# A four-block graph network on one core: offsets loaded one by one eight chunks ahead, ScalarE's share from the fourth group, early counts and weighting on VectorE

## The chip, the core and the metric

One core of one Trainium2 chip. The metric is the device time in microseconds of one execution; for each kernel the median of several runs is given. Engines are called TensorE (PE in the rows; its weight loads PEld), VectorE (DVE), ScalarE (ACT), GpSimd (POOL) and SyncE (SP). Each has a sequencer of its own that takes its instructions in order; rows of a sequencer have a small q behind the engine (PEldq is TensorE's).

## The reference, cut to what matters

x is 512 nodes by 512 features. There are 16384 edges, sorted by dst, each with src, dst, one of 4 types and a weight. Four blocks of graph network follow one another, each in the form x = x + block(relu(layernorm(x))):

```python
h = x @ W + b                                  # block 0, diffusion
adj = 1 where an edge joins two nodes, either way, plus the identity; rows divided by their sum
out = dw[0] * h
for i in range(3):
    cur = adj @ cur                            # cur starts as h
    out = out + dw[i + 1] * cur
return relu(out)
# block 1: per type r: segment_sum((x[src] @ W_rel[r] + b_rel[r]) * weight), two layer norms, a gelu MLP
# block 2: normalised adjacency @ (x @ weight) + bias
# block 3: two SAGE layers, means over incoming edges
```

The edges enter all of this only through five 512 x 512 matrices: for each of the four types the sum of the weights of the edges from one node to another, and the number of edges. Block 0 needs the last one (the counts).

## The kernel before, in words

`build_matrices` turns the edge list into the five matrices in SBUF (`wall`, the counts at index R = 4), and beside that normalises x and multiplies it by block 0's W. `run_blocks` then computes the four blocks. The change lies in the first and at the head of the second.

**Chunks.** The edges are taken in 128 chunks (CH) of 128. As they are sorted by dst, a chunk touches few destination nodes: a window of 8 columns (WIDE) beginning at an offset that the chip works out from the chunk's first dst. VectorE makes, for a group of 16 chunks (G), one-hot matrices by comparison with an iota (`hot`, L375): `lo_hot` (src within its tile of 128), `key_hot` and `cnt_hot` (tile of src, type, and dst within the window). It multiplies `lo_hot` by the weight, which is split into three bf16 parts (V = 3; `weigh`, L381). The one-hots of three groups (RING) fit at a time, so group g waits for the chunks of group g - 3 (`chunk_done`). ScalarE makes the third weighted part for the first 8 chunks (BY_ACT) of groups 1 to 7 (`weigh_some`, L273), 8 activations a group; VectorE does the rest. Group 7 is made in two halves (`last_hots`).

**TensorE, per chunk** (`chunk`, L555): three matmuls with the weighted one-hots as stationary operand (L560, 128 columns) and one with `lo_hot` for the counts (L562, 32 columns). They add into PSUM at a place that is known only at run time: a register holds the chunk's offset, and two register instructions a chunk (FUSED_REGOPS) make the addresses from it. The registers are filled by TENSOR_LOAD instructions that read the offsets from SBUF (`off_row`): before the change one load of 16 registers at the head of each group, L569, eight in all. Behind it on TensorE's sequencer come the waits for the group's one-hots: L578 is the wait on `act_hots_ready`.

**Blocks.** The 512 destination columns lie as 32 blocks of 16 (DB) in the eight PSUM banks, in turn. A block's bank is zeroed by a matmul (L552) when it opens, one every fourth chunk, after its forerunner was copied. ScalarE copies each finished block to `wall` (L279) and its overlap with the next to `tails` (L281), in the order of closing; VectorE adds the tails, four blocks at a time (`add_tails`, L421). The last block is copied by VectorE (L454).

**From counts to hops.** `cnt_r` is a rounded copy of the counts. For the first 384 columns ScalarE makes it (`keep_early_counts`, L267), called between the block copies 28 and 29 in its order, after VectorE's sixth `add_tails` (semaphore `half_built`); the last 128 columns are VectorE's (L500). TensorE adds the counts to their transposes (L623, L617 for the early ones, L629 to L633 for the late). VectorE makes the adjacency of it (`symmetric`, L946), and the hops of block 0 begin (L1116). Before L946, VectorE sums dw (L955), scales b0 by it (L956) and weights the first two tiles of the projection (`weigh_projection`, L950); the other two tiles follow later.

**Order of the start.** VectorE works out keys and offsets, then checks that the edges suit this scheme (L339 to L345; if not, a slow branch with `slow` set runs instead, which these inputs don't take), then takes the moments of the first two tiles of x (`moments`, L312). TensorE turns the plan (L520 to L522) once the checks are done, spins ten matmuls (L507), transposes the first normalised tile (L529), spins six, and multiplies by W (L539; each of the matmuls stands as two rows). Every engine that branches loads the flag first, with a TENSOR_LOAD of one register (L77).

Of the kernel before, what the change touches and what calls it, by code (L numbers as in the profile page):

```python
# [17 lines left out]
F32 = mybir.dt.float32  # L18
# [9 lines left out]
P = 128  # L28
# [17 lines left out]
BY_ACT = 8  # L46
OUT_R = R + 1
# [7 lines left out]
def gnn_program(nc, x_in, src_in, dst_in, typ_in, wgt_in, w0_in, b0_in, dw_in, wself_in, bself_in, wrel_in, brel_in,  # L55
                g1_in, be1_in, g2_in, be2_in, wf1_in, bf1_in, wf2_in, bf2_in, w2_in, b2_in,
                wl1_in, bl1_in, wr1_in, wl2_in, bl2_in, wr2_in, out):
    with ExitStack() as keep:
# [17 lines left out]
        def load_flag(engine, kind):  # L76
# [15 lines left out]
        b0_loaded = sem("b0_loaded")  # L92
        half_built, built, early_kept, late_kept = sem("half_built"), sem("built"), sem("early_kept"), sem("late_kept")
# [4 lines left out]
                       both_ways, bias, inv_cnt, hi[0], lo[0], ident_r, cnt_r, b0, b0_loaded, half_built, built, early_kept, late_kept,  # L98
                       proj_out, hi_ready, lo_ready, sym_ready, x_in, src_in, dst_in, typ_in, wgt_in, w0_in, b0_in)
        run_blocks(nc, sem, block, wall, x, ident, ones, eye, eps, load_flag, psum, slots, h, h_t, adj, cnt_r, both_ways, bias,  # L100
                   inv_cnt, hi, lo, b0, b0_loaded, built, proj_out, hi_ready, lo_ready, sym_ready,
# [5 lines left out]
def build_matrices(nc, sem, sb, block, wall, x, ident, ones, eye, eps, slow_flag, load_flag, banks, psum, slots, h, h_t,  # L107
                   both_ways, bias, inv_cnt, hi0, lo0, ident_r, cnt_r, b0, b0_loaded, half_built, built, early_kept, late_kept,
# [22 lines left out]
    if True:  # L131
# [91 lines left out]
        def _(act):  # L223
# [72 lines left out]
            with act.If_ne(slow, 0):  # L296
                keep_early_counts()

        @block.vector
        def _(dve):  # L300
# [36 lines left out]
            dve.scalar_tensor_tensor(key, high_i, float(R * WIDE) / P, key, ALU.mult, ALU.add).then_inc(keys_ready, 1)  # L337
            dve.wait_ge(const_ready, 1)
# [8 lines left out]
            moments(0)  # L347
            moments(1)
# [5 lines left out]
            scale_and_shift(0)  # L354
# [35 lines left out]
            def hots(g):  # L390
# [8 lines left out]
                weigh(g, V - 1, slice(BY_ACT // 2, G // 2))  # L399
# [15 lines left out]
            def add_tails(q):  # L415
# [6 lines left out]
                                         ALU.add)  # L422

# [6 lines left out]
            with dve.If_eq(slow, 0):  # L430
# [26 lines left out]
            with dve.If_ne(slow, 0):  # L457
# [34 lines left out]
                for m in range(NT):  # L492
                    split_projection(m)
                dve.wait_ge(slow_cnt_out, NT)
# [844 lines left out]
```

## Time and profile before

| | |
|---|---|
| median of 3 runs | 386.02 us (385.9 to 386.74) |
| the profiled execution's own time | 385.97 us |
| its span, first to last instruction | 384.0 us |
| TensorE busy | 366.3 us (95%) |
| VectorE busy | 179.7 us (47%) |
| ScalarE busy | 97.0 us (25%) |
| GpSimd busy | 57.9 us (15%) |
| granted TensorE clock | 0.999 |

The profiled execution lies within 0.1 us of the median; 1.97 us of it lie outside the span. Matmuls are pipelined, so that their rows overlap: the time from one start to the next tells the pace, not the duration of one. Times in rows are microseconds from the start of the span, unless ns is written.

### The profile page before, as it was taken

To read this page: it belongs to the slowest core of one execution; us is meant where nothing else is said; L and a number is where in the kernel's file an instruction comes from. 1 tells how busy PE (TensorE), PEld (TensorE's weight loads), DVE (VectorE), ACT (ScalarE), POOL (GpSimd) and SP (SyncE) were. 2 spreads that over 40 slices of the span, in tenths; PEclk is the share of its full clock that TensorE was granted. 3 is DMA by queue.
4 is the path that set the end of the run, shared out by engine and by line. 5 is a ranking of instruction groups with operands and counts; after the bars stand their busy time and mean duration, and the time that the engine had idled before them with its cause. 6 is when DMAs were issued, how large, how long until landed. Compare 5 with 4: busy or idle time off the path is not lost.

```text
span 384.0 us, 4240 instructions
## 1 busy us (share of the span) xinstructions
PE 366.3 (95%) x1554; PEld 204.5 (53%) x1554; DVE 179.7 (47%) x328; ACT 97.0 (25%) x230; POOL 57.9 (15%) x48
## 2 busy tenths in 40 slices
PE   7898877899999999999999999999999999999996
PEld 2447766788444444454444447544455747445642
DVE  5898998788831122237320332004685447212311
ACT  3449886332510000000000102321124270212000
POOL 5000000000589700010011001000211064000000
PEclk9999999999999999999999999999999999999999
DMA  7000000399100000029100018027333000000011
GB/s 242 32 0 4 2 2 2 131 294 340 59 2 0 0 0 0 0 98 357 66 0 0 2 30 183 6 39 124 58 50 62 0 0 2 0 0 0 2 55 55
DMA packets 43812, 22.05 MB, mean 57 GB/s; under 512 B 35536, under 2 KB 36048, under 8 KB 43792
## 3 DMA queue, kind: packets, MB, share of 16 engines
q1 hardware_dynamic: 43264, 20.85, 19.9%
q0 software_dynamic: 240, 0.79, 0.7%
q8 instruction: 14, 0.23, 0.2%
q10 hardware_dynamic: 288, 0.13, 0.1%
q14 instruction: 6, 0.05, 0.0%
HBM read 20.72 MB, written 1.05 MB: 57 GB/s over the span
## 4 chain that ended last, share of the span: by engine, by line
PE 83%; DVE 12%; ACT 2%; DMA 1%; issue 1%; DVEq 0%; ACTq 0%
PE bank L1116 46%; PE bank L1190 14%; PE bank L1309 7%; PE bank L1221 7%; DVE slots L375 4%; DVE slots L381 3%; PE bank L539 3%; PE bank L1104 2%; PE bank L560 2%; DMA bias<-in_edge_type 1%; PE bank L552 1%; DVE wall L421 1%; DVE stats L922 1%; DVE bias L312 0%; PE bank L1132 0%
## 5 line engine op out<-in xcount | busy, mean ns | idle before, releaser
L1116 PE MATMUL bank<-slots,h_t 128*128 128x512 f32 x192 | 83.6, 593 | 0.8 <-ACT h_t L845 0.8
L1116 PEld LDWEIGHTS bank<-slots,h_t 128*128 128x128 f32 x192 | 35.9, 190 | 43.6 <-issue 43.6
L1190 PE MATMUL bank<-slots,wall 128*128 128x512 f32 x128 | 55.7, 593 | 0.0
L560 PE MATMUL bank<-slots 128*128 128x128 bf16 x384 | 32.6, 220 | 7.5 <-ACT slots L273 4.6
L1190 PEld LDWEIGHTS bank<-slots,wall 128*128 128x128 f32 x128 | 24.0, 190 | 28.7 <-issue 28.7
L997 DVE TENSOR_TENSOR slots<-bank,bias 128x512 f32<-128x512 f32 x16 | 11.1, 691 | 43.9 <-PE bank L1116 43.9
L560 PEld LDWEIGHTS bank<-slots 128*128 128x128 bf16 x384 | 24.8, 97 | 10.9 <-issue 8.4
L1116 PE MATMUL bank<-wall,h_t 128*128 128x512 f32 x64 | 29.0, 593 | 0.5 <-ACT h_t L845 0.5
L1309 PE MATMUL bank<-wall,slots 128*128 128x512 f32 x64 | 28.4, 592 | 0.0
L1116 PE MATMUL bank<-h_t,slots 128*128 128x384 f32 (+2 forms) x96 | 28.0, 451 | 0.0
L1221 PE MATMUL bank<-slots 128*128 128x512 f32 x64 | 27.8, 592 | 0.0
L1116 PE MATMUL bank<-hi,adj 128*128 128x512 f32 x64 | 25.5, 399 | 1.1 <-DVE adj L946 1.1
L1116 PE MATMUL bank<-lo,adj 128*128 128x512 f32 x64 | 24.9, 390 | 0.0
L834 ACT ACTIVATE columns<-mean_var,eps 128x1 f32<-128x1 f32 x20 | 5.9, 293 | 74.7 <-DVE mean_var L923 74.6
L381 DVE TENSOR_TENSOR slots<-slots,inv_cnt 128x2048 bf16<-128x2048 bf16 (+1 forms) x26 | 24.4, 990 | 0.0
L375 DVE TENSOR_TENSOR slots<-inv_cnt,both_ways 128x2048 bf16<-128x2048 f16 (+3 forms) x27 | 21.9, 862 | 2.2 <-PE bank L562 1.7
L562 PE MATMUL bank<-slots 128*128 128x32 bf16 x128 | 22.7, 178 | 0.0
L1116 PEld LDWEIGHTS bank<-h_t,slots 128*128 128x128 f32 x96 | 15.7, 191 | 11.6 <-issue 7.7
L1221 PEld LDWEIGHTS bank<-slots 128*128 128x128 f32 x64 | 12.1, 190 | 14.8 <-issue 14.8
L1309 PEld LDWEIGHTS bank<-wall,slots 128*128 128x128 f32 x64 | 12.1, 190 | 14.5 <-issue 14.4
L1014 DVE SCALAR_TENSOR_TENSOR h<-bank,columns,h 128x512 f32<-128x512 f32 x4 | 3.0, 751 | 35.4 <-PE bank L1190 35.4
L795 POOL TENSOR_TENSOR h<-h,bias 128x512 f32<-128x512 f32 x4 | 5.1, 1264 | 95.2 <-PE bank L1104 95.2
(162 smaller groups left out, 454.6 us busy)
## 6 DMA issues: line engine op xcount, KB each, us to landing
slots<-in_L_gnn_W_rel SPq DMA_DIRECT2D x4, 1024.0 KB, 11.7
slots<-in_L_gnn_W_ffn SPq DMA_DIRECT2D x2, 2048.0 KB, 12.6
slots<-in_L_gnn_Wl SPq DMA_DIRECT2D x32, 64.0 KB, 2.5
slots<-in_L_gnn_Wr SPq DMA_DIRECT2D x32, 64.0 KB, 2.3
x<-in_x SPq DMA_DIRECT2D x4, 256.0 KB, 5.8
bias<-in_L_gnn_W SPq DMA_DIRECT2D x1, 1024.0 KB, 7.9
slots<-in_L_gnn_W_self SPq DMA_DIRECT2D x1, 1024.0 KB, 5.4
bias<-in_L_gnn_b_rel SPq DMA_DIRECT2D x4, 256.0 KB, 10.0
```

What stands on the lines that cost most here:

```text
L375: return dve.tensor_tensor(to[:, pairs], have, want, ALU.is_equal)
L381: dve.tensor_tensor(wgt_hot[:, s, v, pairs], lo_hot[:, s, pairs], by, ALU.mult).then_inc(hots_ready, 1)
L539: ins = pe.matmul(proj_bank[m], h_t[:, k, m * P:(m + 1) * P], w0[:, k, :], start=(k == 0), stop=(k == KT - 1))
L560: pe.matmul(place[:, :, 0:R, 0:WIDE], wgt_hot[:, s, v, a, :, j], key_hot[:, s, a, :, j], start=False, stop=False, skip_group_check=True)
L562: pe.matmul(place[:, :, R, 0:WIDE], lo_hot[:, s, a, :, j], cnt_hot[:, s, a, :, j], start=False, stop=False, skip_group_check=True).then_in ...
L834: act.activation(std[:, t:t + 1], mean_var[:, t, 1:2], ACT.Sqrt, bias=eps[:]).then_inc(std_ready[n], 1)
L997: dve.tensor_tensor(msg[r][:, m, :], main[m][:], brel[r], ALU.add).then_inc(msg_out, 1)
L1104: ins = pe.transpose(t_bank[use % 2][:, i * P:(i + 1) * P], b, ident[:])
L1116: ins = pe.matmul(bank, left, right, start=start and i == 0, stop=stop and i == len(pairs) - 1)
L1190: ins = pe.matmul(main[m][:], wall[:, r, s, tile(m)], msg[r][:, s, :], start=(r == 0 and s == 0), stop=(r == R - 1 and s == NT - 1))
L1221: ins = pe.matmul(main[m][:], hid[:, g, tile(m)], wf2[:, g, :], start=(g == 0), stop=(g == GT - 1))
L1309: ins = pe.matmul(sage_bank[m][:], agg_t[layer][:, k, tile(m)], sage(wl, k), start=False, stop=(k == KT - 1))
```

## The change

- TensorE loads each chunk's offset with a load of its own. The first eight (AHEAD) stand ahead of the first chunk; then the load for chunk c + 8 stands behind the matmuls of chunk c.
- ScalarE makes its part of the weighted one-hots from group 3 on (ACT_FROM); VectorE makes all of groups 0, 1 and 2. TensorE waits for ScalarE's part in groups 3 to 7 alone.
- The early counts' copy moves from ScalarE to VectorE, behind its sixth `add_tails`; the semaphore `half_built` goes.
- Summing dw, scaling b0 and weighting the first two tiles move from the head of `run_blocks` to VectorE's place behind the second `split_projection`, before the seventh `add_tails`. The fourth `split_projection` now follows the third.
- VectorE takes the moments of tiles 0 and 1 before the checks, and `scale_and_shift(0)` before it waits for the turned plan.

```diff
+ACT_FROM = 3
+AHEAD = 8
...
         @block.scalar
...
-            def keep_early_counts():
-                act.wait_ge(half_built, 1)
-                act.activation(cnt_r[:, :, most], wall[:, R, :, most], ACT.Copy).then_inc(early_kept, 1)
...
                 for g in range(1, CH // G + 1):
-                    if g < CH // G:
+                    if ACT_FROM <= g < CH // G:
                         weigh_some(g)
                     while kept < NB - 1 and closes(kept) < g * G:
                         keep_block(kept)
-                        if kept == NB - 4:
-                            keep_early_counts()
                         kept += 1
...
         @block.vector
...
             dve.scalar_tensor_tensor(key, high_i, float(R * WIDE) / P, key, ALU.mult, ALU.add).then_inc(keys_ready, 1)
+            moments(0)
+            moments(1)
             dve.wait_ge(const_ready, 1)
...
-            moments(0)
-            moments(1)
+            scale_and_shift(0)
 
             dve.wait_ge(plan_t_ready, 3)
...
-            scale_and_shift(0)
...
-                weigh(g, V - 1, slice(BY_ACT // 2, G // 2))
+                weigh(g, V - 1, BACK if g >= ACT_FROM else WHOLE)
...
+            def keep_early_counts():
+                dve.tensor_copy(cnt_r[:, :, most], wall[:, R, :, most]).then_inc(early_kept, 1)
+
+            def weigh_bias():
+                dve.wait_ge(dw_loaded, 16)
+                dve.wait_ge(b0_loaded, 16)
+                link(dve.tensor_reduce(dw_sum[:], dw[:], AX.X, ALU.add))
+                link(dve.tensor_scalar(b0[:], b0[:], dw_sum[:], None, ALU.mult))
+
+            def weigh_projection(m):
+                dve.scalar_tensor_tensor(h[:, m, :], h[:, m, :], dw[:, 0:1], b0[:], ALU.mult, ALU.add).then_inc(acc_ready, 1)
...
-                add_tails(NB // 4 - 3).then_inc(half_built, 1)
-                for m in range(NT - 1):
+                link(add_tails(NB // 4 - 3))
+                keep_early_counts()
+                for m in range(2):
                     split_projection(m)
+                weigh_bias()
+                for m in range(2):
+                    weigh_projection(m)
                 add_tails(NB // 4 - 2)
-                split_projection(NT - 1)
+                split_projection(2)
+                split_projection(3)
...
         @block.tensor
...
+            def offset(c):
+
+                return nc.values_load_multi_w_load_instructions(
+                    off_row[0:1, c:c + 1], [PE], min_val=0, max_val=7 * N + DB - 2,
+                    skip_runtime_bounds_check_because="masked to that on the chip")[1][0]
+
...
+                at = [offset(c) for c in range(AHEAD)]
                 for g in range(CH // G):
-                    at = nc.values_load_multi_w_load_instructions(
-                        off_row[0:1, g * G:(g + 1) * G], [PE], min_val=0, max_val=7 * N + DB - 2,
-                        skip_runtime_bounds_check_because="masked to that on the chip")[1]
                     for c in range(g * G, (g + 1) * G):
...
-                            pe.wait_ge(act_hots_ready, BY_ACT * g)
+                            if g >= ACT_FROM:
+                                pe.wait_ge(act_hots_ready, BY_ACT * (g - ACT_FROM + 1))
...
-                        chunk(c, at[c % G])
+                        chunk(c, at[c])
+                        if c + AHEAD < CH:
+                            at.append(offset(c + AHEAD))
...
@@ run_blocks, head of VectorE's program
-            dve.wait_ge(dw_loaded, 16)
-            dve.wait_ge(b0_loaded, 16)
-            dve.wait_ge(proj_out, NT)
-            link(dve.tensor_reduce(dw_sum[:], dw[:], AX.X, ALU.add))
-            link(dve.tensor_scalar(b0[:], b0[:], dw_sum[:], None, ALU.mult))
-            for m in range(2):
-                weigh_projection(m)
             for t in range(NT):
                 symmetric(t)
```

## Rows read from the trace of the kernel before

**Rows 1.** The page's part 4, the chain that ended last, by engine.
```profile
PE 83%; DVE 12%; ACT 2%; DMA 1%; issue 1%; DVEq 0%; ACTq 0%
```

**Rows 2.** Groups by line, TensorE, 28 to 71 us: busy, mean ns, idle before and releasers.
```profile
L560 PE MATMUL bank<-slots 128*128 128x128 bf16 x384 | 32.6, 220 | 7.5 <-ACT slots L273 4.6 <-issue 1.8 <-DVE slots L375 1.1
```

**Rows 3.** TensorE's sequencer by line: ns min/median/max, first and last start; then 42.6 to 45.
```profile
L569 PEldq TENSOR_LOAD <-both_ways x7: 1102/1103/1112, 31.9 to 64.7; - x7
...
L578 PEldq EVENT_SEMAPHORE  x8: 51/51/51, 25.9 to 65.8; - x8
...
L569 PEldq TENSOR_LOAD <-both_ways x1: 1104/1104/1104, 42.7 to 42.7; - x1
...
L578 PEldq EVENT_SEMAPHORE  x1: 51/51/51, 43.9 to 43.9; - x1
...
L560 PEldq FUSED_REGOPS  x3: 42/42/42, 44.0 to 44.5; - x3
```

**Rows 4.** Timeline of TensorE, groups 0 and 7: start us, duration us.
```profile
29.12 0.33 PE L560 MATMUL bank<-slots 128*128 128x128 bf16 x3
...
29.32 0.33 PE L560 MATMUL bank<-slots 128*128 128x128 bf16 x3
...
69.98 0.18 PE L562 MATMUL bank<-slots 128*128 128x32 bf16 x1
...
70.23 0.18 PE L562 MATMUL bank<-slots 128*128 128x32 bf16 x1
```

**Rows 5.** Loads of one register on TensorE's sequencer, the two L77.
```profile
L77 PEldq TENSOR_LOAD <-slow_flag x1: 493/493/493, 23.9 to 23.9; - x1
...
L77 PEldq TENSOR_LOAD <-slow_flag x1: 307/307/307, 72.5 to 72.5; - x1
```

**Rows 6.** Timeline of VectorE, 32 to 70 us.
```profile
32.64 2.70 DVE L375 TENSOR_TENSOR slots<-inv_cnt,both_ways 128x2048 bf16<-128x2048 f16 x3 [1.67 <-PE bank L562]
...
60.29 1.89 DVE L381 TENSOR_TENSOR slots<-slots,inv_cnt 128x1024 bf16<-128x1024 bf16 x3
...
68.92 0.66 DVE L421 TENSOR_TENSOR wall<-wall,bias 128x480 f32<-128x480 f32 x1 [2.99 <-ACT bias L281]
```

**Rows 7.** Timeline of ScalarE, 68 to 71 us.
```profile
68.78 1.49 ACT L267 ACTIVATE cnt_r<-wall 128x1536 fp32r<-128x1536 f32 x1
```

**Rows 8.** The chain that ended last, 72 to 76 us: start, us, what.
```profile
73.03 1.42 DVE h L950 x2
74.45 0.62 DVE adj L946 x2
```

**Rows 9.** Timeline of TensorE, 70 to 76 us.
```profile
70.89 0.41 PE L623 MATMUL bank<-cnt_r,ident_r 128*128 128x384 f32 x1 [0.49 <-issue]
...
72.78 0.50 PE L629 MATMUL bank<-cnt_r,ident_r 128*128 128x128 f32 x3
...
75.11 0.50 PE L1116 MATMUL bank<-hi,adj 128*128 128x512 f32 x1 [1.15 <-DVE adj L946]
```

**Rows 10.** Timeline, 6 to 17 us, and the request of x's second tile.
```profile
6.60 0.69 DVE L312 BATCH_NORM_STATS2 bias<-x 128x6 f32<-128x512 f32 x1
...
8.22 0.25 DVE L352 CAST both_ways<-bank 1x128 int32<-1x128 f32 x1
...
7.21 2.32 PE L507 MATMUL bank<-both_ways 128*128 128x512 bf16 x10
...
11.88 1.96 PE L539 MATMUL bank<-bias,h_t 128*128 128x512 f32 x4 [0.17 <-ACT h_t L235]
...
16.89 1.98 PE L539 MATMUL bank<-bias,h_t 128*128 128x512 f32 x4 [0.90 <-ACT h_t L235]
...
L197 SPq DMA_DIRECT2D x<-in_x x1: 432/432/432, 2.1 to 2.1; - x1
...
DMA to landing us min/median/max: 3.5/3.5/3.5
```

**Rows 11.** Timeline of TensorE, 1 to 5 us.
```profile
1.32 3.48 PE L507 MATMUL bank<-both_ways 128*128 128x512 bf16 x8 [1.32 <-POOL both_ways L205]
```

More of the change, by code:

```diff
@@ L91, in gnn_program @@
         b0 = sb("b0", [P, D], F32)
-        b0_loaded = sem("b0_loaded")
-        half_built, built, early_kept, late_kept = sem("half_built"), sem("built"), sem("early_kept"), sem("late_kept")
+        dw = sb("dw", [P, HOPS + 1], F32)
+        dw_sum = sb("dw_sum", [P, 1], F32)
+        b0_loaded, dw_loaded, acc_ready = sem("b0_loaded"), sem("dw_loaded"), sem("acc_ready")
+        built, early_kept, late_kept = sem("built"), sem("early_kept"), sem("late_kept")
         proj_out, hi_ready, lo_ready, sym_ready = sem("proj_out"), sem("hi_ready"), sem("lo_ready"), sem("sym_ready")
@@ L97, in gnn_program @@
         build_matrices(nc, sem, sb, block, wall, x, ident, ones, eye, eps, slow_flag, load_flag, banks, psum, slots, h, h_t,
-                       both_ways, bias, inv_cnt, hi[0], lo[0], ident_r, cnt_r, b0, b0_loaded, half_built, built, early_kept, late_kept,
+                       both_ways, bias, inv_cnt, hi[0], lo[0], ident_r, cnt_r, b0, dw, dw_sum, b0_loaded, dw_loaded, acc_ready, built, early_kept, late_kept,
                        proj_out, hi_ready, lo_ready, sym_ready, x_in, src_in, dst_in, typ_in, wgt_in, w0_in, b0_in)
         run_blocks(nc, sem, block, wall, x, ident, ones, eye, eps, load_flag, psum, slots, h, h_t, adj, cnt_r, both_ways, bias,
-                   inv_cnt, hi, lo, b0, b0_loaded, built, proj_out, hi_ready, lo_ready, sym_ready,
+                   inv_cnt, hi, lo, b0, dw, dw_loaded, acc_ready, built, proj_out, hi_ready, lo_ready, sym_ready,
                    dw_in, wself_in, bself_in, wrel_in, brel_in,
@@ L107, in build_matrices @@
 def build_matrices(nc, sem, sb, block, wall, x, ident, ones, eye, eps, slow_flag, load_flag, banks, psum, slots, h, h_t,
-                   both_ways, bias, inv_cnt, hi0, lo0, ident_r, cnt_r, b0, b0_loaded, half_built, built, early_kept, late_kept,
+                   both_ways, bias, inv_cnt, hi0, lo0, ident_r, cnt_r, b0, dw, dw_sum, b0_loaded, dw_loaded, acc_ready, built, early_kept, late_kept,
                    proj_out, hi_ready, lo_ready, sym_ready, x_in, src_in, dst_in, typ_in, wgt_in, w0_in, b0_in):
@@ L291, in _ @@
                         keep_block(kept)
-                        if kept == NB - 4:
-                            keep_early_counts()
                         kept += 1
-            with act.If_ne(slow, 0):
-                keep_early_counts()
         @block.vector
@@ L493, in _ @@
                     split_projection(m)
+                weigh_bias()
+                for m in range(2):
+                    weigh_projection(m)
                 dve.wait_ge(slow_cnt_out, NT)
-                dve.memset(stats[:, 0, 0:1], 0.0).then_inc(half_built, 1)
+                keep_early_counts()
                 dve.memset(stats[:, 1, 0:1], 0.0).then_inc(built, 1)
@@ L691, in run_blocks @@
         bf1 = sb("bf1", [P, GT], F32)
-        dw = sb("dw", [P, HOPS + 1], F32)
-        dw_sum = sb("dw_sum", [P, 1], F32)
         dw_inv = sb("dw_inv", [P, HOPS, NT], F32)
@@ L699, in run_blocks @@
         rows_loaded, rel_rows_loaded, late_rows_loaded = sem("rows_loaded"), sem("rel_rows_loaded"), sem("late_rows_loaded")
-        dw_loaded, bf1_loaded = sem("dw_loaded"), sem("bf1_loaded")
+        bf1_loaded = sem("bf1_loaded")
         wself_loaded, w2_loaded = sem("wself_loaded"), sem("w2_loaded")
@@ L722, in run_blocks @@
         inv_root_ready, inv_cnt_ready = sem("inv_root_ready"), sem("inv_cnt_ready")
-        acc_ready, hop_ready = sem("acc_ready"), sem("hop_ready")
+        hop_ready = sem("hop_ready")
         self_ready, self_out, msg_ready, msg_out, agg_ready, agg_out = (
```

2 lines of the change are left out of this document (1 added, 1 removed).

## The prediction

> **What bounds the kernel now.** I read the chain first, for where time can be won or lost at all: TensorE carries 83% of it [rows 1]. The change touches two stretches, the chunk stage (28 to 70 us) and the handover to the hops (70 to 75 us), plus some reordering ahead of 10 us; from 75.11 on nothing changes, so that part only shifts.
>
> In the chunk stage the groups by line show 384 L560 matmuls busy for 32.6 us with 7.5 us of idle before them [rows 2], put down to ScalarE or VectorE. Those two had long been done: the idle sits at each group's start, where TensorE's sequencer loads 16 offsets (L569). From 31.9 on there are seven such loads, 1.103 us each [rows 3]. One boundary tells the rest: load at 42.7 for 1.104 us, then the wait L578 at 43.9, then the register arithmetic (FUSED_REGOPS) of the next chunk at 44.0 [rows 3]. L578 uses none of the loaded registers and its semaphore was satisfied long before, yet it starts only after the load. So **a load holds everything behind it on that sequencer**. From the load's start to the register arithmetic it is 1.3 us; less 1.104 and L578's 0.051 that leaves two steps between instructions of some 0.07 us; I reckon with 0.06.
>
> The sequencer also paces the chunks. In group 0, where it had run ahead while the projections kept the array busy, chunks follow at 0.20 us (29.12, 29.32). In the last group, without zeroing between them, they follow at 0.25 us (69.98, 70.23) [rows 4]. The array needs 0.20, the sequencer 0.25: it has no slack, and whatever is added to it lengthens the stage.
>
> **Offsets one by one.** The change removes 8 loads of 16 registers and adds 128 loads of one. Eight stand ahead of the first chunk and 120 come right behind a chunk's matmuls. "Eight ahead" helps only if the sequencer goes on while a load is under way, which rows 3 speak against. What does a load of one register cost? L77 is one, twice on TensorE's sequencer: 0.493 us at 23.9, the first load of the program there, and 0.307 us at 72.5 [rows 5]. Bounds: below, a cost purely by registers, 1.103/16 = 0.069; above, 0.493. I take 0.307: it is the one that isn't the first of its kind, and a fixed part with a rate per register fits both sizes (0.307 + 15 x 0.053 = 1.10). With the step of 0.06 behind it a load adds 0.365 us, and a chunk goes from 0.25 to 0.61 us.
>
> The sum goes along the sequencer:
> - Leading loads: today's first starts near 24.7 (L578's first, 25.9, less one load and a step [rows 3]); 8 x 0.365 = 2.9 from there, to 27.6. The projections hold the array until 28.2, so they are covered; if they weren't, they would cost the difference to today's single load, 1.8 us.
> - First 16 chunks: 16 x 0.61 = 9.8 and some 0.1 for the zeroing, to 37.5. Today it is through with them at 31.9, and with the load and the wait behind it at 33.1: +4.4 us.
> - The other 112 chunks: 104 more loads x 0.365 = 38.0, less six removed loads of 1.16 = 7.0, less 0.2 for the waits L578 of groups 1 and 2: +30.8 us.
> - Together **+35.2 us**: the last chunk ends near 105.6 instead of 70.4.
>
> The ends of the price for a load: at 0.069 the 128 loads give 30.5 us less (390 in all), at 0.493 they give 23.8 more (444).
>
> The Trainium skill (DMA: Bandwidth & Descriptors, Latency and other measured facts) gives a floor of about 600 ns for a tensor_load. By it the time would be an estimated 458 us; the trace disagrees, with 307 and 493 ns for the same thing, and the rows decide.
>
> **ScalarE's share from group 3.** VectorE weighs the front half of groups 1 and 2 too: 2 x 0.6 us (three products take 1.89 at half size [rows 6]). It then stood idle for 1.67 us before group 3, waiting for chunks [rows 6]: covered today, and by far with chunks at 0.61. ScalarE loses 16 small activations in time that it doesn't need. Worth 0 here; without that cover it would be +1.2.
>
> **Early counts.** ScalarE's copy L267 (1.49 us at 68.78) held up the last two block copies [rows 7]. It goes to VectorE, which waited 2.99 us before 68.92 [rows 6]. No row has this form on VectorE: bounds 1.5 (what ScalarE takes) to 2.1 (L421, 0.66 for 480 elements a partition [rows 6], for 1536), both below 2.99, and the wait grows with slow chunks. Cost 0. The last block's tail is then added a little earlier, but TensorE's own work (L623, L617: 70.89 to 72.78 [rows 9]) is ready no sooner, being released by the end of the chunks and not by the counts.
>
> **Weighting early.** The bias scaling and two L950 (73.03 for 1.42 us) stand right before the first L946 in the chain [rows 8]. They move into VectorE's wait. L946 then waits for the first L629, which starts at 72.78 (three in 0.50 us [rows 9]): it starts at about 73.1 instead of 74.4. **-1.3 us**, bounds 0 (if the moved work lay exposed in its new place) and -1.6 (nothing between L500 and L946). Late next is L629, behind TensorE's counts. b0 and dw were asked for in the first microseconds, long before: no wait.
>
> **Moments before the checks.** VectorE does the two moments (6.60 to 8.22, 1.6 us [rows 10]) before the checks. x's second tile was asked for at 2.1 and took 3.5 to land: by 5.6, in time for its moments near 6.2. But the plan's matmuls wait for the checks, and behind them on TensorE are ten spins and the first transposes. Spins at 7.21 become 8.8 and the first L539 at 11.88 about 13.1. Four plus four of them with the transposes between take 4 us, so the second tile, today waiting 0.90 us for h_t until 16.89, starts at 17.05: **+0.2 us** (bounds -0.15 and +1.2).
>
> **Sum.** 35.2 - 1.3 + 0.2 = +34.1. The profiled execution took 385.97 (span 384.0, 1.97 outside it), level with the median of 386.02. Forecast **420 us**.
>
> **Rivals.**
> 1. *The load runs beside what follows* and only the use of the register waits; eight chunks ahead hides it. Then VectorE bounds: from 32.64 it works without a break until the last half group at 62.1 [rows 6], eight chunks of 0.25 end at 64.1, not 70.4. -6.3 - 1.3 + 0.2 = -7.4: 378.6 us. It decides the sign where a load holds the sequencer for less than 0.078 us (the 9.4 us otherwise saved, over 120). For it: the program is plainly written for that. Against it: L578 lies behind the load all eight times (25.9 to 65.8 [rows 3]). If a load still takes a step of 0.1, the time is about 389. Chance 0.10, of which 0.07 faster, 0.01 the same. The Trainium skill (Advanced Engine Details and Errata, Sequencer Loop) says that other engine instructions can be read and queued while a control instruction executes, which read widely is this rival; no row here shows it, since a chunk begins with register arithmetic, no engine instruction.
> 2. *A load is priced by its registers*: 0.07 to 0.2 us, 390 to 405 us. Against it: 0.307 for one register. Chance 0.04.
> 3. *TensorE's clock falls to 1.2 GHz*, as its array works 0.20 of each 0.61 us. Spins took 0.43 us each at the start (3.48 for 8) and 0.23 later (2.32 for 10) [rows 10, 11]. In the chunk stage 0.40 is still under 0.61; the count transposes (1.9 us) would double and the first hops run at half speed: +2 to +4, 422 to 424. It lies within the forecast, a quarter of it.
>
> The forecast's case, with a load between about 0.2 and 0.5 us, has 0.84; 0.02 is left for what I don't see, counted as slower but 0.01.
>
> **Numbers.** Range 410 to 440: a load of 0.23 (420 - 10) up to 0.46 (420 + 20), the clock included; outside lie rivals 1 and 2 and the outer price. Less than 0.2%, 0.8 us, can't be told from no change. Faster 0.07, same 0.02, slower 0.91.
>
> **What would show it.** 128 one-register loads near 0.31 us, register arithmetic 0.06 behind each; chunks 0.61 apart from the first to the 120th and 0.25 for the last eight; no pause at group boundaries; ScalarE and VectorE waiting on L562 throughout; TensorE idle two thirds of the stage; first hop 3.4 us behind the last chunk's end (70.4) where it was 4.7 (75.11 [rows 9]). Wrong if FUSED_REGOPS starts while a load is still open: then the stage is shorter than today's, VectorE has no idle in it, and rival 1 holds.

## The result, and the profile after

The changed kernel takes 422.91 us (median of 4 runs, 421.57 to 423.35) where the kernel before takes 385.96 in the same comparison: 1.0946 times as long, interval 1.0917 to 1.0976. The forecast was 420, range 410 to 440. The profiled execution took 421.57 us, its span 419.5, at a mean granted TensorE clock of 0.909 (before: span 384.0, 0.999). It is the fastest of the four: the median lies 1.3 us above it, and no trace shows where those are spent.

The page of the kernel after: part 1, the granted clock in 40 slices of part 2, and the chain by engine (rows 1 showed TensorE 83% and VectorE 12%).

```profile
PE 403.2 (96%) x1554; PEld 224.0 (53%) x1554; DVE 182.2 (43%) x329; ACT 91.9 (22%) x213; POOL 57.9 (14%) x48
...
PEclk9997555555899999999999999999999999999999
...
PE 93%; DVE 2%; issue 2%; ACT 1%; DMA 1%; ACTq 0%
```

VectorE has all but left the chain. The slices are 10.5 us wide: in the fifth to tenth, 42 to 105 us, the granted clock is half of full speed. That is nearly the whole chunk stage.

TensorE's sequencer, the loads by line over the whole run, then between 60 and 61.9 us, with the register arithmetic of the same stretch (ns min/median/max, first and last start):

```profile
L572 PEldq TENSOR_LOAD <-both_ways x128: 293/298/313, 25.4 to 103.8; - x128
...
L572 PEldq TENSOR_LOAD <-both_ways x3: 298/298/307, 60.2 to 61.4; - x3
...
L581 PEldq FUSED_REGOPS  x3: 42/42/42, 60.5 to 61.8; - x3
```

They alternate. Three loads start within 60.2 to 61.4, so one starts every 0.60 us, and the register arithmetic of a chunk (at 60.5 behind the load of 60.2) starts after each. The same stretch on the array, to be set against the pace of 0.25 in [rows 4]:

```profile
60.03 0.50 PE L581 MATMUL bank<-slots 128*128 128x128 bf16 x3
60.33 0.23 PE L583 MATMUL bank<-slots 128*128 128x32 bf16 x1
60.64 0.50 PE L581 MATMUL bank<-slots 128*128 128x128 bf16 x3
60.93 0.23 PE L583 MATMUL bank<-slots 128*128 128x32 bf16 x1
61.24 0.50 PE L581 MATMUL bank<-slots 128*128 128x128 bf16 x3
```

A chunk starts every 0.60 us. The groups by line and the waits of the stage, 28 to 108 us (waits: us in total, times, longest), say who follows whom:

```profile
L581 PE MATMUL bank<-slots 128*128 128x128 bf16 x384 | 58.6, 295 | 7.5 <-issue 3.6
...
ACT wall L279 <- PE bank L583: 47.8, 26, 3.0
DVE slots L370 <- PE bank L583: 23.1, 5, 6.8
PEld bank L581 <- issue: 18.5, 63, 0.4
```

ScalarE waits 47.8 us and VectorE 23.1 us for chunks to end; the weight loads wait 18.5 us for issue, that is, for nothing but their own sequencer. In the row of matmuls TensorE looks almost as busy as ever: idle before them is 7.5 us, the same as in [rows 2], and busy time has grown from 32.6 to 58.6. That is the trap of this profile. The matmuls are no more work; each is shown longer (295 ns against 220) at the lower clock, and the pipelined rows fill the gap that the loads make. The pace, not the busy share, shows the loss.

The last of the register arithmetic of the chunks, before (its L560) and after:

```profile
L560 PEldq FUSED_REGOPS  x128: 42/42/42, 26.0 to 69.9; - x128
```

```profile
L581 PEldq FUSED_REGOPS  x128: 42/42/42, 28.4 to 105.9; - x128
```

The sequencer reaches the last chunk 36.0 us later. At the end of the stage, the answer to [rows 9]:

```profile
106.95 0.23 PE L583 MATMUL bank<-slots 128*128 128x32 bf16 x1
107.02 0.67 PE L645 MATMUL bank<-cnt_r,ident_r 128*128 128x384 f32 x1
...
109.33 0.50 PE L651 MATMUL bank<-cnt_r,ident_r 128*128 128x128 f32 x3
...
110.40 0.50 PE L1129 MATMUL bank<-hi,adj 128*128 128x512 f32 x1
```

The last chunk ends at 107.18 (before 70.41) and the first hop starts at 110.40 (before 75.11): 3.22 us between them where there were 4.70. From the last chunk, +36.8, the handover gives back 1.5; 35.3 us are left at the first hop, and the span is 35.5 us longer.

### The profile page after: what moved, and what is told of

Its sections match the earlier page's. It is cut to its first block, busy times and chain, and to the rows that moved or that the text cites. A ratio compares the mean times of both kernels' runs of the same rounds, so it can differ in the third digit from the quotient of the medians.

```text
span 419.5 us, 4340 instructions
## 1 busy us (share of the span) xinstructions
PE 403.2 (96%) x1554; PEld 224.0 (53%) x1554; DVE 182.2 (43%) x329; ACT 91.9 (22%) x213; POOL 57.9 (14%) x48
## 4 chain that ended last, share of the span: by engine, by line
PE 93%; DVE 2%; issue 2%; ACT 1%; DMA 1%; ACTq 0%
PE bank L1129 42%; PE bank L1203 13%; PE bank L581 12%; PE bank L1322 7%; PE bank L1234 7%; PE bank L567 4%; PE bank L554 3%; PE bank L1117 2%; PE bank L522 1%; DMA bias<-in_edge_type 1%; PE bank L583 1%; DVE stats L942 1%; PE bank L544 0%; PE bank L1145 0%; PE bank L639 0%
## 5 line engine op out<-in xcount | busy, mean ns | idle before, releaser
L581 PE MATMUL bank<-slots 128*128 128x128 bf16 x384 | 58.6, 295 | 7.5 <-issue 3.6
L1129 PEld LDWEIGHTS bank<-slots,h_t 128*128 128x128 f32 x192 | 35.9, 190 | 43.6 <-issue 43.6
L581 PEld LDWEIGHTS bank<-slots 128*128 128x128 bf16 x384 | 33.4, 123 | 24.0 <-issue 18.5
L370 DVE TENSOR_TENSOR slots<-inv_cnt,both_ways 128x2048 bf16<-128x2048 f16 (+3 forms) x27 | 21.9, 863 | 23.7 <-PE bank L583 23.1
L583 PE MATMUL bank<-slots 128*128 128x32 bf16 x128 | 28.7, 224 | 0.0
L376 DVE TENSOR_TENSOR slots<-slots,inv_cnt 128x2048 bf16<-128x2048 bf16 (+1 forms) x26 | 25.5, 1033 | 0.0
L279 ACT ACTIVATE wall<-bank 128x320 f32<-128x320 f32 x31 | 13.4, 434 | 47.8 <-PE bank L583 47.8
```

The source lines that it names most:

```text
L279: act.activation(wall[:, :, :, b * DB:(b + 1) * DB].rearrange("p r t d -> p t r d"), block_of(b)[:, :, :, 0:DB], ACT.Copy).then_inc(block_ ...
L370: return dve.tensor_tensor(to[:, pairs], have, want, ALU.is_equal)
L376: dve.tensor_tensor(wgt_hot[:, s, v, pairs], lo_hot[:, s, pairs], by, ALU.mult).then_inc(hots_ready, 1)
L581: pe.matmul(place[:, :, 0:R, 0:WIDE], wgt_hot[:, s, v, a, :, j], key_hot[:, s, a, :, j], start=False, stop=False, skip_group_check=True)
L583: pe.matmul(place[:, :, R, 0:WIDE], lo_hot[:, s, a, :, j], cnt_hot[:, s, a, :, j], start=False, stop=False, skip_group_check=True).then_in ...
L1129: ins = pe.matmul(bank, left, right, start=start and i == 0, stop=stop and i == len(pairs) - 1)
```

## The experiments

The theory after the result: a load of one register holds TensorE's sequencer for 0.30 us and a step of 0.06, whatever is behind it and however far off its use. The rivals: the loss lies in another part of the change; the distance of eight chunks hides some of it; the lower clock makes it. Every kernel was compared with the kernel before on the same chip, whose medians lay between 385.96 and 386.11.

### Which part of the change costs it

The kernel after with only the loads of 16 registers back at the heads of the groups:

```diff
...
-                at = [offset(c) for c in range(AHEAD)]
+                cuts, at = [0, 16, 32, 48, 64, 80, 96, 112, 128], []
...
+                        if c in cuts:
+                            at += offsets(c, cuts[cuts.index(c) + 1] - c)
...
-                        if c + AHEAD < CH:
-                            at.append(offset(c + AHEAD))
```

> The changed kernel with the eight loads of 16 registers back at the groups' heads; all other parts of the change stay. Theory (a load holds TensorE's sequencer, the rest of the change is worth little): the chunk stage is back near 42 us, the handover keeps its 1.3 us gain, the start keeps the 0.8 us that the spins at half clock cost: 385.4 us, between 384.5 and 386.2. Rival (something else of the change, ScalarE's share or VectorE's added work, lengthens the stage): over 395 us.

Measured 386.35 us, 1.0004 times the kernel before (0.9992 to 1.0017): just above the range that was expected, and the rival, over 395, is out. And the other way round, the kernel before with nothing but the loads changed (edit as in the diff of the change: `offset`, the eight ahead, one behind each chunk):

> The kernel before with only the loads changed: one register each, eight chunks ahead. Theory: all of the loss is here. 120 chunks at 0.60 us in place of 0.25 and the 16-register loads gone: +36 us on the sequencer and about 0.8 for the array at half clock behind it: 422.5 us, between 421 and 424. Rival (the loss needs the other parts too): under 400 us.

Measured 422.29 us, 1.0938 (1.0917 to 1.0959). So all of the loss lies in the loads. Everything else in the change together makes no difference that these runs can tell from none, where 1.1 us had been forecast as its gain.

### Whether the distance hides anything

The kernel after with `AHEAD = 1` in place of 8:

> The changed kernel with AHEAD = 1: each offset is loaded one chunk ahead instead of eight. Theory (the sequencer stands still during a load, so the distance to its use hides nothing): the same time, 421.5 to 423. Rival (the load runs on its own, and the distance hides part of it): each chunk would wait for up to 0.25 us more, 452 us.

Measured 427.12 us (424.65 to 429.46), 1.1081. The total is a miss, but not by way of the distance. The register arithmetic of the chunks in this kernel:

```profile
L581 PEldq FUSED_REGOPS  x128: 42/42/42, 24.3 to 105.6; - x128
```

Its last starts at 105.6, with eight ahead at 105.9. The ends alone prove little, since the stage starts earlier here (zeroing at 27.41, not 28.93) and holds seven more loads. What decides is the pace: between 40 and 100 us both sequencers start 95 loads, so **the chunks come as fast without any distance**. The time is lost behind the stage. With eight ahead the last eight chunks have no load and follow more closely; with one ahead they too are 0.60 apart. In windows behind the stage (us; busy time and count of PE, PEld, DVE, ACT, POOL; granted clock; DMA share; GB/s) it shows:

```profile
106.00:109.00 3.00, 2.63 (x14) 2.47 (x12) 1.45 (x3) 0.60 (x2) 0.00 (x0) 0.50 0.21 17
109.00:112.00 3.00, 3.00 (x14) 2.90 (x15) 1.36 (x5) 0.00 (x0) 0.00 (x0) 0.50 0.92 325
112.00:116.00 4.00, 4.00 (x13) 3.23 (x13) 3.42 (x11) 0.00 (x0) 0.00 (x0) 0.61 1.04 291
```

and the same place in the kernel after:

```profile
104.00:108.00 4.00, 3.93 (x40) 3.78 (x37) 2.44 (x5) 1.81 (x6) 0.00 (x0) 0.51 0.01 4
108.00:112.00 4.00, 4.00 (x28) 3.68 (x27) 3.24 (x9) 0.00 (x0) 0.00 (x0) 1.00 0.51 187
```

At 1.2 GHz (0.50) through the count transposes and at 0.61 in the first hops, where the kernel after is back at 1.00 from 108 on. Its first hop starts at 112.10 instead of 110.40. The profiled execution (424.65) is the fastest of the four, so the trace says nothing on the 2.5 us between it and the median.

Then each offset loaded twice, with both registers in use (the second for the chunk's count matmul):

```diff
-            def chunk(c, at):
+            def chunk(c, at, again):
...
-                pe.matmul(place[:, :, R, 0:WIDE], lo_hot[:, s, a, :, j], cnt_hot[:, s, a, :, j],
+                pe.matmul(counted[:, :, R, 0:WIDE], lo_hot[:, s, a, :, j], cnt_hot[:, s, a, :, j],
...
+                            at.append(offset(c + AHEAD))
+                            twice.append(offset(c + AHEAD))
```

> The kernel before with one-register loads eight chunks ahead, each offset loaded twice: the first register addresses the three weighted matmuls, the second the counts' matmul, so that both loads are needed and both are far ahead of their use. Theory (a load holds the sequencer for 0.30 us and a step of 0.06 however far its use is): 120 x 0.36 = 43 us on top of only_loads (422.3): 465 us. Rival (what costs is waiting for the value, not the load): 422 to 425 us.

Measured 467.14 us (465.78 and 468.51), 1.2089 (1.2041 to 1.2137). The loads in it:

```profile
L558 PEldq TENSOR_LOAD <-both_ways x248: 294/302/313, 24.6 to 147.0; - x124
```

120 more loads than in the kernel that changes the loads alone, and the profiled execution is 43.6 us longer than that one's (465.78 against 422.16): 0.363 us a load, against 0.365 in the sum.

An earlier attempt at this, with a second load whose result nothing used:

> The kernel before with one-register loads eight chunks ahead, and behind each of the 120 a second load of one register that nothing uses. Theory (a load costs its 0.30 us and a step of 0.06 whether or not its value is waited for): 120 x 0.36 = 43 us on top of the kernel with the loads alone, 465 us. Rival (only the use of the register waits): about the same as with the loads alone, 422 us.

It took 423.24 us and is void: its trace has 128 loads of offsets, as many as without the edit, so the unused ones never ran. It says nothing on either theory.

### Whether an engine instruction can pass a load

The prediction's rival 1 had one reading that no row before could exclude: behind a load there was always register arithmetic or a semaphore, never an engine instruction alone. So the kernel before, with the load for chunk c + 8 between the first and the second matmul of chunk c. The weight load of the second matmul has a fixed address and needs no register.

```diff
+                    if v == 0 and c + AHEAD < CH:
+                        ahead.append(offset(c + AHEAD))
```

> As only_loads, but the load for chunk c + 8 stands between the first and the second matmul of chunk c. Theory (nothing behind a load is handed on before it ends, engine instructions included): the weight loads of the second matmul begin only after the load's end, some 0.35 us behind the first's; time 422 us as only_loads, or up to 1 us more. Rival (matmuls can be handed on while a load is under way): the second and third matmul follow the first at 0.06 to 0.11 us inside the load's duration, and the stage is up to 0.05 us a chunk shorter: 416 to 420 us.

Its profiled execution took 423.89 us; the other one took 437.77, far outside what these kernels otherwise scatter, and I draw nothing from it. The first is 1.7 above the profiled execution of the kernel that changes the loads alone, where at most 1 was expected and the rival wanted less time, not more. Two of its loads, and the weight loads in the same stretch (start us, us):

```profile
L558 PEldq TENSOR_LOAD <-both_ways x1: 299/299/299, 60.4 to 60.4; - x1
...
L558 PEldq TENSOR_LOAD <-both_ways x1: 299/299/299, 61.1 to 61.1; - x1
```

```profile
60.40 0.14 PEld L567 LDWEIGHTS bank<-slots 128*128 128x128 bf16 x1
60.73 0.14 PEld L567 LDWEIGHTS bank<-slots 128*128 128x128 bf16 x2 [0.19 <-issue]
60.88 0.10 PEld L571 LDWEIGHTS bank<-slots 128*128 128x128 bf16 x1
61.08 0.10 PEld L567 LDWEIGHTS bank<-slots 128*128 128x128 bf16 x1
61.44 0.14 PEld L567 LDWEIGHTS bank<-slots 128*128 128x128 bf16 x2 [0.25 <-issue]
```

The load of 60.40 lasts 0.30 us, and the next weight load starts at 60.73; the load of 61.1 is over at 61.41, and the next starts at 61.44. Before both the weight loads stand idle, 0.19 and 0.25 us, for nothing but issue. The whole trace agrees: of the 117 loads of offsets that start after 29.5 us, one has a weight load that starts inside it, 2 ns after its own start. So nothing new is handed to the array while a load is open; in the kernel after matmuls do start beside a load, but they stand ahead of it in the program. The Trainium skill (Advanced Engine Details and Errata, Sequencer Loop) says that other engine instructions can be queued while a control instruction executes; for a register load on TensorE this trace disagrees.

### What the lower clock costs

The kernel after with one matmul of zeros, 440 columns wide, added to the banks for each chunk below 112. It leaves the sums as they are and keeps the array busier without touching the loads.

```diff
+                if c < CH - G:
+                    pe.matmul(flat[:, bass.ds(at, NT * OUT_R * COLS)], zeros[:, 0:P], zeros[:, 0:NT * OUT_R * COLS],
+                              start=False, stop=False, skip_group_check=True)
```

> The changed kernel with one more matmul per chunk, for chunks 0 to 111: zeros by zeros, 440 columns, added at the chunk's place, so that TensorE's array works 0.38 of each 0.60 us instead of 0.20. Theory (the clock fell because the array idled behind the loads, and costs only the lag of the last chunks and the slow start of the handover, 1.1 us): granted clock at least 0.98 over the span, 440-column matmuls 0.18 us apart from what follows, 421 to 424 us, the gain of 1.1 given back by one more instruction a chunk. Rival (the clock falls all the same): 0.76 us of array work a chunk, 437 us or more.

Measured 422.02 us (421.6 to 423.74), 1.0935 (1.0899 to 1.0971). The stage in windows, first of the kernel after, then of this one:

```profile
28.00:40.00 12.00, 9.47 (x85) 6.13 (x84) 5.25 (x7) 3.08 (x9) 0.00 (x0) 0.84 0.00 1
40.00:52.00 12.00, 10.94 (x82) 7.48 (x81) 7.44 (x9) 5.17 (x18) 0.00 (x0) 0.50 0.01 2
```

```profile
28.00:40.00 12.00, 11.37 (x101) 6.98 (x100) 5.24 (x7) 3.08 (x9) 0.00 (x0) 1.00 0.01 1
40.00:52.00 12.00, 11.11 (x100) 6.83 (x101) 7.41 (x9) 4.97 (x18) 0.00 (x0) 1.00 0.01 2
```

With the array given more to do, the clock stays at 2.4 GHz (1.00) and the time is the same. So the clock fell because the array had so little to do between loads: here it fell at a pace of 0.60 us a chunk, and at the same pace with the added matmul it did not.

What its fall costs is small, and the medians (0.9 us apart, the runs of each spread over 2 us) can't tell it from nothing. In the traces the last register arithmetic of a chunk starts 0.9 us later than in the kernel after (106.8 against 105.9), which is the price of the added instructions, and yet the array ends the stage at the same time (107.24 against 107.18). So the low clock cost about 0.8 us there: the half-speed matmuls still fit between two loads, and only the last chunks lag.

### What the rest of the change is worth

The kernel after with the old loads, and the moments back behind the checks (the handover's edits kept):

```diff
-            moments(0)
-            moments(1)
             dve.wait_ge(const_ready, 1)
...
-            scale_and_shift(0)
+            moments(0)
+            moments(1)
 
             dve.wait_ge(plan_t_ready, 3)
...
+            scale_and_shift(0)
```

> The changed kernel with loads of 16 back and also the old order at the start (the checks before the moments of tiles 0 and 1, scale_and_shift(0) after the plan's copies). Left of the change: ScalarE's share from group 3, the early counts on VectorE, the early weighting. Theory (these give 1.3 us at the handover, and the new order at the start was what gave it back): 384.7 us, between 384.2 and 385.2. Rival (the start's order is worth nothing, and something else eats the 1.3 us): 386 us.

Measured 384.78 us, 0.9961 (0.9945 to 0.9978): 1.3 us faster than the kernel before. The handover here takes 3.37 us from the last chunk's end to the first hop, by its trace.

The opposite, the kernel before with only the moments ahead of the checks:

> The kernel before with only the new order at the start: the moments of tiles 0 and 1 ahead of the checks, scale_and_shift(0) ahead of the plan's copies. Theory (TensorE waits 1.6 us longer for the plan, its spins behind that wait run at half clock, and the first projection starts 1 to 3 us later, of which the second tile's wait for h_t absorbs a part): 1.6 us slower, as undo_loads stood to old_front: 387.6 us, between 387.0 and 388.1. Rival (the sum of the prediction, spins at full clock, +0.2): 386.2 us.

Measured 387.99 us, 1.0033 (1.0015 to 1.0051). Its runs spread from 386.50 to 388.90: the medians are 2.0 us apart, the ratio of all runs gives 1.3. The timeline of its TensorE, to be set against [rows 10], where ten spins took 2.32 us and the first projection started at 11.88:

```profile
7.93 0.37 PE L520 MATMUL bank<-ident,bias 128*1 128x128 f32 x1 [1.57 <-DVE bias L347]
...
8.81 4.43 PE L507 MATMUL bank<-both_ways 128*128 128x512 bf16 x10
...
15.06 1.45 PE L539 MATMUL bank<-bias,h_t 128*128 128x512 f32 x3
```

The plan's matmul waits 1.57 us for VectorE's checks, now behind the moments, and the ten spins after it run at half speed, 0.44 us each. The zeroing of the chunk stage then starts at 30.11 instead of 28.17. The change's two parts that look like reordering thus work against each other: the handover gives 1.3 us, the start takes 1.3 to 2.

### A version that is faster than both

Three more kernels start from the one with the old front. The first loads fewer times: 32 and 16 registers ahead of the first chunk, then 32, 32 and 16 at chunks 48, 80 and 112.

```diff
-                cuts, at = [0, 16, 32, 48, 64, 80, 96, 112, 128], []
+                cuts, at = [0, 48, 80, 112, 128], []
...
-                            at += offsets(c, cuts[cuts.index(c) + 1] - c)
+                            if c == 0:
+                                at += offsets(0, 32)
+                            at += offsets(len(at), cuts[cuts.index(c) + 1] - len(at))
```

> As old_front, with 5 loads of 32, 16, 32, 32 and 16 registers: the first two ahead of the first chunk, the others at chunks 48, 80 and 112. Theory (a load holds the sequencer for 0.245 us and 0.053 per register, and the sequencer sets the stage's pace): loads of 1.94 us; the first two end at 27.9 while the projections still hold the array, the other three cost 5.2 where seven cost 8.1: 3.0 us faster than old_front, 381.7 us. Rival 1 (the stage is set by VectorE once the pauses shrink): 384.7, as old_front. Rival 2 (a load costs by its registers alone): no gain but the covered one, about 383.

Measured 383.83 us, 0.9934 (0.9914 to 0.9954): faster than the old front, by 1 us only where 3 were expected. A load of 32 registers takes 2.14 us where 1.94 was reckoned, hardly less than two of 16. And with the last chunk ending at 68.81 VectorE has become late (a load at 40.8 and one at 51.8, and the copy of the last block):

```profile
L572 PEldq TENSOR_LOAD <-both_ways x2: 2138/2138/2139, 40.8 to 51.8; - x2
```

```profile
70.31 0.48 DVE L466 COPY wall<-bank 128x320 f32<-128x320 f32 x1
```

This trace is of the slowest of seven executions (385.85 us). In it the granted clock is 0.52 from 55 to 58 us, behind the pause of the load at 51.8, 1.00 at the end of the stage (66 to 68.8), 0.84 in the handover (68.8 to 73.7) and 0.72 in the first hops (73.7 to 77).

The next keeps 16 registers a load and puts the first three loads ahead of the first chunk, where the projections hold the array anyway:

```diff
-                cuts, at = [0, 16, 32, 48, 64, 80, 96, 112, 128], []
+                cuts, at = [0, 48, 64, 80, 96, 112, 128], []
...
-                            at += offsets(c, cuts[cuts.index(c) + 1] - c)
+                            while len(at) < cuts[cuts.index(c) + 1]:
+                                at += offsets(len(at), G)
```

> As old_front, but the first three loads of 16 stand ahead of the first chunk; the others stay at the heads of groups 3 to 7. Theory (the projections cover 3.4 us of loads, and two pauses of 1.16 us go; a pause of 1.1 us leaves the clock up, where the 2.1 us ones of few_loads let it fall in some executions): the chunk stage ends 2.3 us earlier. VectorE, whose work ahead of the last block's copy ends at 70.4 in few_loads, is then late and takes back half: 383.5 us, between 382.4 and 384.2. Rival (VectorE isn't the next bound): 382.4 us. Other rival (the pauses were covered anyway): 384.8 us.

Measured 383.99 us, 0.9936 (0.9914 to 0.9958). The last chunk ends at 68.56 instead of 70.10, but the copy of its block comes 1.3 us later than that, behind two splits of the projection:

```profile
68.67 1.28 DVE L434 TENSOR_TENSOR lo<-h,hi 128x512 fp32r<-128x512 f32 x2
69.88 0.48 DVE L466 COPY wall<-bank 128x320 f32<-128x320 f32 x1
```

This too is the slowest execution of its kernel (385.38 us; the others took 383.65 to 384.25): TensorE waits 0.42 us for VectorE's copy of the counts, the granted clock is 0.64 from 71 to 74 us, and the first hop starts at 73.22.

So the last kernel moves those two splits behind the adjacency of their tiles in `run_blocks`:

```diff
-                split_projection(2)
-                split_projection(3)
...
@@ run_blocks, VectorE, behind the adjacency of tile t
+                if t >= 2:
+                    dve.tensor_tensor(lo[0][:, t, :], h[:, t, :], hi[0][:, t, :].bitcast(F32), ALU.subtract).then_inc(lo_ready, 1)
```

> As three_first, but the splits of projection tiles 2 and 3 (two operations of 0.6 us on VectorE ahead of the last block's copy) stand behind the adjacency of tiles 2 and 3. Theory (in three_first VectorE sets the handover: it is 1.3 us late with the last block's copy): the copy starts within 0.2 us of the last chunk's end, TensorE's counts are then the last to be ready, the first hop starts 1.1 us earlier and some 0.3 us of that is lost to hop rows 2 and 3 waiting for their splits: 383.2 us, between 382.8 and 383.7. Rival (VectorE's lateness was covered by TensorE's counts): 384.0 us, as three_first.

Measured 383.60 us (383.51 to 384.28), 0.9924 (0.9896 to 0.9951): **2.5 us faster than the kernel before and 39 faster than the changed one.** It has the lowest median of the three, but the three intervals overlap, so that it beats the other two is not shown by the times. VectorE, with the copy at once behind the last chunk, which ends at 68.61:

```profile
68.68 0.49 DVE L464 COPY wall<-bank 128x320 f32<-128x320 f32 x1
...
71.23 0.69 DVE L965 SCALAR_TENSOR_TENSOR adj<-bank,eye 128x512 fp32r<-128x512 f32 x1 [0.81 <-PE bank L650]
```

The first hop then starts at 71.98, with the clock still at 1.00.

## Why the prediction was right, step by step

**What a load holds up.** Right, and it is the whole result. L578 behind the loads of 16 [rows 3] was the right row to argue from: loading one by one beside the kernel before costs 36.3 us (422.29 less 386.03), the distance of eight hides nothing (95 loads in 60 us with either), and with a load between two matmuls the second waits for the load's end.

**The price of a load.** Taken 0.307 + 0.06; measured 0.298 and, from start to start, 0.60 for a bare chunk where 0.61 was said. The choice of the second L77 over the first [rows 5] was right. The sequencer's end of the stage was to come 35.2 later; it came 36.0 later, and 0.8 of that is the later start of the stage (below). The eight leading loads were covered, as said: 25.4 to 28.3, while the last projections still run.

**A term that was missing.** The array ends 0.8 us further behind its sequencer than before (36.8 against 36.0), because the last eight chunks, without loads, are now paced by an array at 1.2 GHz: 0.35 us a chunk, not 0.25. With the clock kept up they were 0.25 apart again (the kernel with the zeros). The rows of the kernel after:

```profile
106.32 0.48 PE L581 MATMUL bank<-slots 128*128 128x128 bf16 x3
...
106.67 0.48 PE L581 MATMUL bank<-slots 128*128 128x128 bf16 x3
```

**The clock (rival 3).** It did come true: granted 0.50 from 40 to 107 us. Its price in the kernel after was put at 2 to 4 us, for transposes and first hops at half speed. It is nearer 1, by the traces of the kernels with and without the zeros: the clock was back at 1.00 from 108 on, ahead of most of the handover. The price of 2 to 4 fits the kernel that loads one ahead, where the clock stays down through the handover (3.1 us more in the profiled execution). The prediction gave this rival a quarter and left it out of the central sum; it should have been the likelier case, since it had counted that the array works a third of the time. The range had room for its price; the central sum left the mechanism out.

**Early counts at 0, ScalarE's share at 0.** Right. The counts' copy takes 0.96 us on VectorE, less than both bounds (1.5 to 2.1): the conversion by ScalarE's duration and by L421 [rows 6] were both too dear. It runs in a wait of 8.8 us for the block's tail, and the weighting behind it:

```profile
94.72 0.66 DVE L416 TENSOR_TENSOR wall<-wall,bias 128x480 f32<-128x480 f32 x1 [8.83 <-ACT bias L281]
95.42 0.96 DVE L420 CAST cnt_r<-wall 128x1536 fp32r<-128x1536 f32 x1
...
98.20 1.41 DVE L429 SCALAR_TENSOR_TENSOR h<-h,dw,b 128x512 f32<-128x512 f32 x2
```

**Weighting early, -1.3.** Right, by rows and not by a run of its own: 4.70 us became 3.22, and 3.37 with the old loads, where the cover is VectorE's old wait alone. What is late next was right too: VectorE's adjacency waits for the transposed counts (L651 at 109.33, L966 at 109.64).

**Moments first, +0.2.** The step that was mis-sized. Up to the spins the moves came out somewhat better than said: they were forecast for 8.8 and started at 8.31. But ten spins took 3.85 us, not the 2.32 of [rows 10], so the first projection started at 13.88, not 13.1. The rows of the kernel after:

```profile
7.83 0.27 PE L535 MATMUL bank<-ident,bias 128*1 128x128 f32 x1 [1.78 <-DVE bias L342]
...
8.31 3.85 PE L522 MATMUL bank<-both_ways 128*128 128x512 bf16 x10
```

The stage's zeroing starts at 28.93 instead of 28.17, so +0.8 in this execution. With one load ahead the order of the start is the same, but the spins ran at full speed:

```profile
8.17 2.32 PE L522 MATMUL bank<-both_ways 128*128 128x512 bf16 x10
```

There the first projection starts at 12.06 and the zeroing at 27.41, 0.76 earlier than in the kernel before. In the old order slow spins do no harm: with the old front they took 4.00 us and the zeroing still started at 28.09, because the second tile's wait for h_t (0.90 [rows 10]) absorbs them. So the edit does two things: it takes that wait away, worth 0.8, and with it the slack behind which slow spins were hidden. What it is worth hangs on the spins, from -0.8 to +1.9 in these traces (+1.9 in the kernel before with this edit alone). The prediction had the half-speed spins in [rows 11] and used them for the stage alone.

**The sum.** +0.8 start, +35.2 loads, +0.8 array lag, -1.5 handover, and 0.2 behind the first hop make 35.5, the difference of the spans; forecast +34.1. The 35.2 is what is left of the sequencer's 36.0 when the 0.8 is taken off. The median is 2.9 us above the forecast of 420, and 1.3 of that is the distance from the profiled execution to the median. One bound of rival 2 was off by 1: a load of 0.2 us gives 406, not 405. The chance of 0.91 for slower and the low chance for rivals 1 and 2 rested on rows that held.

**What would show it.** All signs came but two. The last eight chunks were 0.35 us apart, not 0.25. And "TensorE idle two thirds of the stage" doesn't show in the rows, which have it busy for 10.94 of 12 us at the half clock. The sign should have been the pace of the chunks and the granted clock.

Open: merging the two register operations of a chunk, which would give the sequencer back its slack, was not tried. Nor do the runs settle what brings the half-speed spins. With the moments first they came in four of five traces (the ten took 3.85 us in the kernel after, 4.43 with the old loads, 4.43 with the moments alone, 3.51 with the zeros), behind pauses of 1.38 to 1.84 us, but not with one load ahead (2.32 behind 1.53). With the old order they came in four of nine (4.00 with the old front, 3.84 and 3.70 in the next two kernels, 3.67 with the loads alone), behind pauses of at most 0.83, and not in the other five (2.32 each). The pause before the plan can't be the whole cause: in five of these eight traces the matmul ahead of it was slow already, as in the kernel before with the moments alone, where L517 took 0.42 us at 5.93, against 0.27 in the kernel before. So the new order makes slow spins costly; that it makes them more frequent is not shown.

## What to carry to other kernels

On TensorE's sequencer a register load is a blocking call in every kernel here; no run tried another engine. Count loads times (fixed part + registers x rate) as if it were compute, and don't expect a distance between load and use to hide any of it. Where a sequencer already paces the stage (here 0.25 us a chunk against 0.20 in the array), load many registers at once (16 took 1.10 us, sixteen loads of one would take 16 times 0.36), and put loads where the array has a backlog. Before moving work ahead of something that others wait for, ask what slack that wait was hiding. After a change that thins out TensorE's work, look at the granted clock at the stage's end and not at the busy share: what matters is whether it is back up when the next bound stage starts.

## What the runs showed of the hardware

- A load on TensorE's sequencer took 0.298 us for one register, 1.103 for 16 and 2.138 for 32: 0.054 us a register up to 16, 0.065 from there. The first load of the program there took 0.493.
- It took the same whether its register was used one chunk later or eight, and whether it stood behind the chunk or inside it.
- TensorE's granted clock went from 1.00 to 0.50 in a stage in which a load stands between any two chunks and the array is given work again every 0.60 us. In the kernel with the loads alone it was back at 1.00 for a short stretch in between (55.2 to 58 us). With a matmul of zeros added to each chunk, at the same pace, it stayed at 1.00.
- In these traces the distance mattered in one way: with eight ahead, the last eight chunks come without loads, and the clock was up again at 108 us; with one ahead, of which there is one trace, it was still at 0.50 at 112, and the first hop started 1.7 us later. In the other traces with eight ahead it was at 1.00 too when the first hop started.
